# Four transformer layers on one core: where the expert bias is added, how many batches the router ranks at once, and when the third layer's weights are loaded

## What is computed

```
layer 0   x = x + mha(ln(x), ln(x));  x = x + mha(ln(x), ln(ctx))         16 heads of 16
          h = ln(x);  logits = h @ router_w.T + router_b
          vals, idx = top_k(logits, 2);  gates = softmax(vals)            8 experts
          eo[e] = gelu(h @ fc1[e].T + fc1_b[e]) @ fc2[e].T + fc2_b[e]     256 -> 1024 -> 256
          x = x + sum over the two chosen e of gates[e] * eo[e]
layer 1   the 10 best rows of a batch by x @ score_w attend to ctx and are replaced
layer 2   grouped-query attention (16 heads of 64, 4 key heads), then silu(x Wg) * (x Wu) Wd
layer 3   x = x + mha(ln(x), ctx) with weights rounded to three values
```

## Time and profile before

| | |
|---|---|
| median of 3 runs | 1499.87 us (1491.66 to 1502.2) |
| the profiled execution, its own time | 1505.26 us |
| its span, first to last instruction | 1503.5 us |
| granted TensorE clock, mean | 0.919 of full speed |
| PE busy / DVE / ACT / POOL | 87% / 47% / 42% / 28% |

### The profile page before, as it was taken

One profiled execution on the slowest core, in us unless ns is written; L12 is line 12 of the kernel. 1 busy time (PEld: TensorE's weight loads), 2 busy tenths in 40 slices (PEclk: granted clock), 3 DMA queues, 4 the chain that ended last, 5 costly groups with the idle time before them and its releaser, 6 DMA issues. The chain is left out here.

```text
span 1503.5 us, 32899 instructions
## 1 busy us (share of the span) xinstructions
PE 1301.7 (87%) x13090; PEld 1046.5 (70%) x13090; DVE 702.6 (47%) x1511; ACT 629.7 (42%) x1558; POOL 428.0 (28%) x569
## 2 busy tenths in 40 slices
PE   3899999974799999992666669999999999868997
PEld 1666666653699999992443457888888888755665
DVE  3677777766231000003555435544546454335666
ACT  2444455321245554440222216555646555325442
POOL 5223336246400000003333024342424333142200
PEclk9999999975699999996777769999999999989999
DMA  9910000003589999993100000000000000000000
GB/s 351 414 59 2 2 2 2 16 30 114 188 298 337 318 322 334 329 307 94 29 28 28 0 1 2 1 2 2 2 1 1 2 1 2 1 1 1 16 16 30
DMA packets 83184, 138.44 MB, mean 92 GB/s; under 512 B 5336, under 2 KB 63712, under 8 KB 83040
## 3 DMA queue, kind: packets, MB, share of 16 engines
q1 hardware_dynamic: 78672, 127.02, 24.0%
q0 software_dynamic: 3072, 8.39, 1.7%
q10 hardware_dynamic: 1296, 1.02, 0.2%
HBM read 107.32 MB, written 29.10 MB: 91 GB/s over the span
## 5 line engine op out<-in xcount | busy, mean ns | idle before, releaser
L1353 ACT ACTIVATE w_ca<-scores,fc1b 128x128 f32<-128x128 f32 x312 | 114.3, 367 | 137.5 <-PE scores L1309 116.2
L868 ACT ACTIVATE reg<-scores 128x1024 f32<-128x1024 f32 x96 | 93.0, 1021 | 151.5 <-PE scores L657 151.2
L1309 PEld LDWEIGHTS scores<-reg 128*128 128x128 f32 x1248 | 146.7, 193 | 4.5 <-issue 2.6
L1309 PE MATMUL scores<-reg 128*128 128x128 f32 x1248 | 147.2, 277 | 2.1 <-issue 1.1
L1319 PE MATMUL bank<-reg,w_ca 128*128 128x256 f32 x624 | 141.1, 379 | 0.3 <-DVE small L1366 0.3
L938 DVE TENSOR_REDUCE reg<-scores 128x8 f32<-128x1024 f32 x96 | 113.0, 1219 | 57.8 <-PE scores L647 57.6
L1804 ACT ACTIVATE reg<-reg,mx 128x128 f32<-128x128 f32 x256 | 99.1, 389 | 83.8 <-DVE mx L1984 83.5
L1374 DVE COPY reg<-bank 128x256 f32<-128x256 f32 x39 | 16.6, 425 | 238.5 <-PE bank L1319 238.4
L1893 POOL TENSOR_TENSOR reg<-reg,rden 128x512 f32<-128x512 f32 x64 | 66.6, 1040 | 210.8 <-DVE rden L1989 210.7
L1319 PEld LDWEIGHTS bank<-reg,w_ca 128*128 128x128 f32 x624 | 115.6, 190 | 14.5 <-DVE small L1366 0.3
L1720 PE MATMUL scores<-reg 128*128 128x128 f32 x1024 | 122.4, 279 | 0.5 <-ACT reg L1827 0.5
(11 more groups left out here) (258 smaller groups left out, 2393.7 us busy)
## 6 DMA issues: line engine op xcount, KB each, us to landing
reg<-in_fc SPq DMA_DIRECT2D x78, 1024.0 KB, 7.2
expert_rows<-reg SPq DMA_DIRECT2D x36, 480.0 KB, 14.6
reg<-expert_rows SPq DMA_DIRECT2D x39, 128.0 KB, 5.4
expert_rows<-reg SPq DMA_DIRECT2D x39, 128.0 KB, 6.3
xres<-in_x SPq DMA_DIRECT2D x1, 2048.0 KB, 11.5
ctxr<-in_ctx SPq DMA_DIRECT2D x1, 2048.0 KB, 8.4
w_l<-in_w_l SPq DMA_DIRECT2D x2, 1024.0 KB, 6.5
out<-xres SPq DMA_DIRECT2D x8, 256.0 KB, 2.1
```

Of the source, the lines that this page charges most:

```text
L868: ins = nc.scalar.activation(PT2[:, t % 2, 2 * half:2 * half + 2, :, :, :].rearrange("p r s c q -> p (r s c q)"), scores4[:, 2 * half:2 * ...
L1309: ins = nc.tensor.matmul(S[n % 4][:, 0:P], up_w8[j % 2][:, c, f * P:(f + 1) * P], xbT[:, j % 2, c, :], start=(c == 0), stop=(c == C - 1))
L1353: nc.scalar.activation(h1[:, j % 2, f, :], S[n % 4][:, 0:P], ACT.Gelu, bias=fc1b[:, bass.ds(e * FC + f, 1)]).then_inc(M["fc1_free"], 1)
```

## The change

It has three parts.

1. **The bias.** `fc2b` is loaded as a table of 128 equal rows (1 MB instead of 8 KB). In the experts' block DVE reads the pass's expert into a register and adds the expert's bias to the 128 result rows where it only copied them. The gate turns, the bias matmuls, their copies on ACT and the eight additions on DVE are gone.
2. **The router.** Ranks, choices, counts and places are made for sets of batches, (0, 4), (4, 4), (8, 4), (12, 2), (14, 2), as (first, number), and `scatter` issues a set's indirect DMAs together. The slots of `turn` and `logits` move. In a slot PE now does `turn` ahead of `logits` and `count`, and the bank for these two is number 5 instead of 7 from slot 27 on. The normalized rows lie in a place of their own (`routed`), where layer 2's weights lay, and no longer in those of layers 1 and 3.
3. **The loads.** The weights of layers 1 and 3 are loaded at the start of the kernel, those of layer 2 (5.5 MB) in the first block of layer 1, behind the mask; and their multiplication with the gains on POOL moves from the experts' block to the fourth group of layer 1, behind that group's last scaling.

```diff
@@ loads @@
         def load_the_rest(sp):
             sp.dma_start(ctxr[:], A["ctx"].rearrange("b p d -> p b d")).then_inc(ld["ctx"], 16)
-            sp.dma_start(w_ca[:], A["w_ca"].rearrange("(c p) n -> p c n", p=P)).then_inc(ld["ca"], 16)
+            for n, t in (("ca", w_ca), ("l1", w_l1), ("l3", w_l3)):
+                sp.dma_start(t[:], A["w_" + n].rearrange("(c p) n -> p c n", p=P)).then_inc(ld[n], 16)
             for k in range(ZEROS):
                 sp.dma_start(xs_dram.rearrange("(p r) d -> p (r d)", p=P)[:, k * ZN:(k + 1) * ZN], zeros)\
                     .then_inc(ld["zeros"], 16)
+            sp.dma_start(down_bias, A["fc2b"]).then_inc(ld["fc2b"], 16)
+
+        def load_grouped(sp):
             for n, t in (("wq2", wq2), ("wkv2", wkv2), ("wo2", wo2), ("wg2", wg2), ("wu2", wu2), ("wd2", wd2)):
                 sp.dma_start(t, A[n].rearrange("(c p) n -> p c n", p=P)).then_inc(ld["l2"], 16)
@@ attention, homes of the banks @@
-                if routed("count", t) + routed("logits", t):
-                    in_c.append(("re", t))
                 in_c += [("rx", q) for q in routed("turn", t)]
+                if has_results(t):
+                    (in_c if t < 27 else in_b).append(("re", t))
@@ attention, PE @@
-                        if routed("count", t) + routed("logits", t):
+                        for q in routed("turn", t):
+                            router.turn_rows(pe, claim_home(pe, ("rx", q)), q).then_inc(full(("rx", q)), 1)
+                        if has_results(t):
                             bank = claim_home(pe, ("re", t))
                             for q in routed("logits", t):
                                 await_moved(pe, ("rx", q))
                                 ins = router.logits(pe, bank, q)
-                            for q in routed("count", t):
-                                ins = router.count(pe, bank, q)
+                            for k in routed_sets("count", t):
+                                ins = router.count(pe, bank, k)
                             ins.then_inc(full(("re", t)), 1)
-                        for q in routed("turn", t):
-                            router.turn_rows(pe, claim_home(pe, ("rx", q)), q).then_inc(full(("rx", q)), 1)
...
                         router.totals(pe, claim_home(pe, ("rt", 0))).then_inc(full(("rt", 0)), 1)
-                        router.pe_gates(pe)
@@ Router @@
             slots = {
                 "stats": [20, 22, 24, 26, 28, 30, 32, 34],
-                "turn": [23, 25, 27, 29, 31, 33, 34, 35],
-                "logits": [24, 26, 28, 30, 32, 34, 35, 36],
-                "choose": [25, 27, 29, 31, 33, 34, 35, 36],
-                "count": [26, 28, 30, 32, 34, 36, 36, 37],
-                "place": [27, 29, 31, 33, 35, 36, 36, 37],
+                "turn": [23, 24, 25, 27, 29, 31, 33, 35],
+                "logits": [26, 26, 28, 28, 32, 32, 34, 36],
             }
+            sets = [(0, 4), (4, 4), (8, 4), (12, 2), (14, 2)]
+            set_slots = {
+                "rank": [26, 28, 32, 34, 36],
+                "choose": [27, 29, 32, 34, 36],
+                "count": [28, 30, 33, 35, 37],
+                "place": [28, 30, 33, 35, 37],
+            }
@@ Router, ranks @@
+                own_logits = logit[:, b0:b0 + n, :]
+                others = own_logits.unsqueeze(2).to_broadcast([P, n, E, E])
...
+                link(nc.vector.tensor_reduce(set_rank[:, 0:n, :], above_k, AX, ALU.add))
@@ Router, scatter @@
+                for b in range(b0, b0 + n):
+                    for s in range(2):
+                        nc.gpsimd.indirect_dma_start(xs_dram, bass.IndirectOffsetOnAxis(pick_row[:, s, b:b + 1], 0),
+                                                     routed[:, b, :], None).then_inc(M["scattered"], 16)
@@ experts, DVE @@
                 dve.wait_ge(ld["l3"], 16)
+                dve.wait_ge(ld["fc2b"], 16)
...
-                    nc.vector.tensor_copy(yb[:, j % 2, :], T[j % 2][:, 0:D]).then_inc(M["y_ok"], 1)
+                    e = dve.value_load(block_expert[0:1, j:j + 1], min_val=0, max_val=E - 1)
+                    nc.vector.tensor_tensor(yb[:, j % 2, :], T[j % 2][:, 0:D], down_bias[:, bass.ds(e * D, D)], ALU.add)\
+                        .then_inc(M["y_ok"], 1)
@@ layer 1, first block, SP @@
                 sp.dma_start(mask2, A["mask"].rearrange("b q k -> q b k")).then_inc(ld["mask"], 16)
+                load_grouped(sp)
@@ best_tokens, POOL @@
                     for n in range(4):
                         pool_scale(pool, n)
+                    if last:
+                        pool.wait_ge(ld["l2"], 16 * 6)
+                        for w, gain in ((wq2, "ln1"), (wkv2, "ln1"), (wg2, "ln2"), (wu2, "ln2")):
+                            for c in range(C):
+                                nc.gpsimd.tensor_scalar(w[:, c, :], w[:, c, :], col(gain, c), None, ALU.mult)
```

More of the change, by code:

```diff
@@ L540, in routed, with routed_sets, has_results @@
                 return [] if router is None else [q for q, at_slot in enumerate(router.slots[step]) if at_slot == t]
-            END = LAST if router is None else router.slots["place"][-1] + 1
+            def routed_sets(step, t):
+                return [] if router is None else [k for k, at_slot in enumerate(router.set_slots[step]) if at_slot == t]
+            def has_results(t):
+                return routed("logits", t) + routed_sets("count", t)
+            END = LAST if router is None else router.set_slots["place"][-1] + 1
             in_a, in_b, in_c = [], [], []
@@ L903, in _ @@
                             router.centre(pool, link, q)
-                        for q in routed("place", t):
-                            router.scatter(pool, q)
+                        for k in routed_sets("place", t):
+                            router.scatter(pool, k)
                     if router is not None:
@@ L966, in _ @@
                                 ins = router.take_logits(dve, bank, q)
-                            for q in routed("count", t):
-                                ins = router.take_places(dve, bank, q)
+                            for k in routed_sets("count", t):
+                                ins = router.take_places(dve, bank, k)
                             ins.then_inc(free(("re", t)), 1)
@@ L999, in _ @@
                             router.stats(dve, link, q)
-                        for q in routed("logits", t):
+                        for k in routed_sets("place", t):
+                            await_moved(dve, ("re", router.set_slots["count"][k]))
+                            router.places(dve, link, k)
+                        for k in routed_sets("rank", t):
                             await_moved(dve, ("re", t))
-                            router.ranks(dve, link, q)
-                        for q in routed("choose", t):
-                            router.choose(dve, link, q)
-                        for q in routed("place", t):
-                            await_moved(dve, ("re", router.slots["count"][q]))
-                            router.places(dve, link, q)
+                            router.ranks(dve, link, k)
+                        for k in routed_sets("choose", t):
+                            router.choose(dve, link, k)
                     if router is not None:
@@ L1132, in count @@
-            def count(self, pe, bank, q):
-                pe.wait_ge(M["chosen_ok"], q + 1)
-                pair = slice(2 * q, 2 * q + 2)
-                to = bank[:, 2 * E + 16 * (q % 2):4 * E + 16 * (q % 2)]
-                nc.tensor.matmul(to, later, chosen[:, pair, :].rearrange("p b e -> p (b e)"), start=True, stop=False)
-                return nc.tensor.matmul(to, ones[:, :], chosen_before[:, pair, :].rearrange("p b e -> p (b e)"),
-                                        start=False, stop=True)
@@ L1140, in places @@
-            def places(self, dve, link, q):
-                pair = slice(2 * q, 2 * q + 2)
-                for k, mask in enumerate((first, second)):
-                    link(nc.vector.tensor_tensor(pair_part, pair_at[:, q % 2, :, :], mask[:, pair, :], ALU.mult))
-                    link(nc.vector.tensor_reduce(pair_total, pair_part, AX, ALU.add))
-                    ins = nc.vector.tensor_copy(pick_row[:, k, pair], pair_total)
-                    if k == 0:
+                own_logits = logit[:, b0:b0 + n, :]
@@ new lines, in count @@
+            def count(self, pe, bank, k):
+                b0, n = self.sets[k]
+                pe.wait_ge(M["chosen_ok"], k + 1)
+                own = slice(b0, b0 + n)
+                to = bank[:, 4 * E:4 * E + n * E]
+                nc.tensor.matmul(to, later, chosen[:, own, :].rearrange("p b e -> p (b e)"), start=True, stop=False)
+                return nc.tensor.matmul(to, ones[:, :], chosen_before[:, own, :].rearrange("p b e -> p (b e)"),
+                                        start=False, stop=True)
@@ new lines, in take_places, with places @@
```

(13 more changed lines are left out.)

132 lines of the change are left out of this document (46 added, 86 removed).

## The result

The changed kernel took **1511.2 us** (median of 8 runs, 1507.8 to 1513.0), the kernel before 1499.3 in the same comparison (8 runs, 1491.7 to 1502.2): ratio **1.0087** (95%: 1.0063 to 1.0112), 11.9 us slower. I had said 1498 (a little faster), and 1484 to 1512. The profiled execution of the changed kernel took 1511.3 us, its span is 1509.5.

A forecast was written before the change was run, and what follows sets the result against it. It took chains of short steps to set the pace around the experts, and PE to bind the experts. Terms -12.7 - 1.7 + 0.4 + 3.3 + 8.8 gave -1.9 us, hence 1498 against the median 1499.9, range 1484 to 1512.

The forecast's parts named there:

- The block's end, -12.7: End of the attention block: experts start at P + 53.3 instead of P + 66.0, 12.7 us less.
- P: End of the attention block's last value products, 331.0 us in the earlier profile; later steps are counted from it.
- a rival as a possible gain: Clock stays up in slots 28 to 33, and DVE's late count may not come again: 1486 us; 17%.
- P itself, -1.7: Slots up to the last value products: bank, slot 30, ranks and turns together save 1.7 us, between -6 and +6.
- my 2.0 for all of them: Turns one slot behind their statistics wait for POOL in slots 25 to 31: +2.0 us beyond what ranks cover.
- The bank and slot 30: Logits no longer wait for bank 7 in slots 28, 30, 32: -4.2 us; no logits in slot 30: -1.5.
- The experts, +0.4: Experts' block: bias addition and register load are covered by PE's work except at the end of pass 39: +0.4 us.
- The gathers, +3.3: Layer 1's first block: gathers land later beside 6.5 MB of loads, +3.3 us, ends 0 and +5.
- The fourth group, +8.8: Layer 1's fourth group: POOL's eight multiplications, 20.1 us, end at 888.5 instead of the block's 879.7: +8.8 us.
- The start, 0: Start of the kernel: loads lose 5.5 MB and gain 3, nobody waits for them: 0 us.
- the block's end doesn't move as counted: Rival: scatters and row loads keep their time, experts start at 386.4, nothing won in P: 1502 us; 12%.
- turns that hold PE and a falling clock: Rival: turns in slots 25 to 31 wait the full 1.9 us, PE falls to half clock: 1512 us; 16%.

The follow-up runs named there:

- the second profile: At P + 53.6, the changed kernel rerun unchanged: 1521.6 us, ratio 1.0072; at the late count, the kernel before rerun unchanged: 1501.4 us.
- before's second profile: The kernel before, run and profiled once more with no edit: 1501.4 us.
- the last two: The kernel before profiled a third time, 1509.5 us, and the changed kernel a second time, 1521.6 us (ratio 1.0072), both without edits.
- split form: Against the kernel with DVE multiplications and layer 2's loads behind the gathers: pair 7's normalization between the third set's fourth and fifth scatters; 1491.2 us, 0.9943; again 0.9971.

## Why the prediction was wrong, step by step

- **The block's end, -12.7: the step that failed.** From P to the experts it had taken 66.0 us, and was to take 53.3. The second number was right: pair 7's normalization ended at P + 24.8 (I said 25.1), the tables came at P + 37.2 (37.4), the experts at P + 52.7 (53.3; in the second profile P + 53.6), P being 334.8. The first, the base, was wrong. The 66.0 us of the earlier trace rows held stalls: the count that DVE got late (3.4 more than in the second profile) and the gates (6.9). Against that one profile the term came out, 66.0 less 52.7; without stalls before's experts start at P + 55.8 (389.76 less 333.96), and the term is **-3.1**. The late count I had seen, and given to a rival as a possible gain; I should have taken it out of the base of the sum.
- **Two errors inside it cancelled, and that is luck.** SP's loads don't need 10.2 us behind the tables, but 5.3 (371.97 to 377.3); the 10.2 held the same kind of delay (5.5 in before's second profile). What holds the experts is a wait that I didn't have, for the 4 MB of weights ahead of the rows, which end near 387.
- **P itself, -1.7: +1.7 without stalls, +12.4 with them.** From slot 24 to P it was 60.7 us in before's second profile and 62.4 in the changed kernel, 61.5 and 73.9 in the last two. The turns waited for POOL as feared, 1.1 us in slot 27 and 3.0 in slot 31; my 2.0 for all of them was half. The bank and slot 30, for which I took off 5.7, have no experiment of their own; with the whole router as before it was 60.8 us from slot 24 to P. That eight scatters in a row could hold up the slots beside them I didn't think of. So where the stalls are, the first term is near mine (65.0 less 53.6, 11.4 us), and the second eats it.
- **The experts, +0.4**: -0.4 and +0.5 by the two pairs of profiles, those without stalls and those with them, 7.24 us a pass as said.
- **The gathers, +3.3: right, 3.6** (2.7 in the last two profiles, 2.9 by undoing). By the Trainium skill's rule (DMA: Bandwidth & Descriptors, Queues, rings and completion order) I had put it nearer 5; the traces lie at 2.7 to 3.6, so they don't bear that price out.
- **The fourth group, +8.8: right, 9.7**, and by the trace all of it came back with the multiplications on DVE.
- **The start, 0**: slot 24 begins at 268.3, 273.3 and 271.7 us in three profiles of before, so the 4.1 us by which the first trace of before and that of the changed kernel differ are not the change's.

With the first two terms as measured without stalls the sum is -3.1 + 1.7 - 0.4 + 3.6 + 9.7 = +11.5; the medians differ by 11.9. So close a fit is partly chance: the two traces as wholes (before's second, the changed kernel's first) differ by 9.9, since the stages without a term give another -1.6, and executions of one kernel differ by several us. Of the rivals, "the block's end doesn't move as counted" (12%) came nearest in kind, since it had the loads as the bound. That 1511.2 lies within 1484 to 1512 at all is luck as well: the upper end stood for turns that hold PE and a falling clock, and the turns took only 2 us over what I had counted.

## What to carry to other kernels

Before a term is built on one profile, look in it for waits without a releaser and for late counts; a base that holds 10 us of them makes a change of that stage look 10 us better. A removed piece of work is worth only the time up to what is late next: the gates were worth some 3 us in one order and over 7 in another. And work that is moved away from its cover costs what sticks out of the new one: 9.7 of the eight multiplications' 20 us on POOL and none on DVE, which had room, and 3 us for 5.5 MB of loads, none once they stood behind the gathers.

## What the runs showed of the hardware

In two batches (before at 1510 us) and in the first profile of before, PE, ACT and DVE stood still for some 1 to 7 us at a time beside or just behind indirect DMAs that POOL issued, and SP issued its weight loads late (the fourth 9.5 to 10.2 us behind the tables in the kernel before, instead of 5.5). In nine profiles from other runs of the same and related kernels, with scatters at the same place, none of this is found. In the kernels that issue four scatters in a row, slots 24 to 31 took 66 to 68 us with stalls and 60 to 63 without; in those that issue eight, 74 to 77 and 62 to 65. Why is open. It is not a fixed trait of a chip, if the record's numbers mean what they say: chip 9 stands there for a batch with stalls and for one without. Separately, two executions of the kernel before differed by 5 us up to slot 10 (145.8 and 150.8 us): in the short one the granted clock was 1.00 from 50 to 80 and from 110 to 145 us, in the long one 0.94 and 0.95. They also differed by 4.4 us in layers 2 and 3, again the second one the longer; why is not shown.

The best orders beat both kernels, by 0.2 to 0.6%: pairs with the bias and the multiplications on DVE and the late loads (0.9944 with stalls, 0.9983 without), and sets with pair 7 brought forward (0.9951 and 0.9950 with stalls; in its split form 0.9971 with and 0.9943 without).
